# The state-space stage of a four-stage layer chain: one activation table set, the token sum on GpSimd, and five call lists in a new order

## The reference

```python
A = -jnp.exp(A_log)
zxbcdt = u @ W_in.T
z = zxbcdt[..., :D_INNER]
xBC = zxbcdt[..., D_INNER:D_INNER + CONV_DIM]
dt = jax.nn.softplus(zxbcdt[..., D_INNER + CONV_DIM:] + dt_bias)
xBC = _silu(conv over 4 tokens of xBC + conv_b)
...
xs = x * dt;  Ad = A * dt
Y_diag = einsum(C, B, exp(segsum(Ad)), xs)
states = running state, decayed by exp(cumsum(Ad)), plus B, xs
y = Y_diag + Y_off + x * D
y = y * _silu(z)
y = y * lax.rsqrt(jnp.mean(y * y, axis=-1, keepdims=True) + EPS) * norm_w
return y @ W_out.T
```

## Time and profile before

| what | value |
|---|---|
| median of 3 runs | 1187.65 us |
| lowest and highest | 1184.77 and 1187.85 us |
| the profiled execution: time | 1185.47 us |
| its span in the trace | 1183.4 us |
| PE busy in the span | 1045.4 us, 88% |
| DVE | 959.9 us, 81% |
| ACT | 893.4 us, 75% |
| POOL | 738.1 us, 62% |
| first layer, start to end | 0 to 359.8 us |

### The profile page before, as it was taken

One profiled execution on the slowest core, in us unless ns is written; L12 is line 12 of the kernel. 1 busy time (PEld: TensorE's weight loads), 2 busy tenths in 40 slices (PEclk: granted clock), 3 DMA queues, 4 the chain that ended last, 5 costly groups with the idle time before them and its releaser, 6 DMA issues. The chain is left out here.

```text
span 1183.4 us, 17445 instructions
## 1 busy us (share of the span) xinstructions
PE 1045.4 (88%) x5234; PEld 698.0 (59%) x5234; DVE 959.9 (81%) x1319; ACT 893.4 (75%) x1697; POOL 738.1 (62%) x638
## 2 busy tenths in 40 slices
PE   5999999999968999998476599999999999988987
PEld 4677677676753334444245357667575766756576
DVE  5999999999962576545689989999999999999741
ACT  7878787887644455556777889999898999986743
POOL 1546554654560443534568997979889897988420
PEclk9999999999998999999678899999999999999899
DMA  4543434323405001112866546556565565645201
GB/s 128 153 135 109 122 104 130 112 82 114 126 29 180 1 18 54 37 36 91 211 137 172 123 136 150 143 135 149 151 143 139 151 158 135 148 133 142 67 5 36
DMA packets 93232, 133.83 MB, mean 113 GB/s; under 512 B 8786, under 2 KB 47698, under 8 KB 93140
## 3 DMA queue, kind: packets, MB, share of 16 engines
q1 hardware_dynamic: 93140, 132.73, 41.6%
HBM read 116.45 MB, written 14.16 MB: 110 GB/s over the span
## 5 line engine op out<-in xcount | busy, mean ns | idle before, releaser
L2219 DVE TENSOR_TENSOR_SCAN state<-bank_a,h,state 128x512 f32<-128x512 f32 x256 | 316.4, 1270 | 27.5 <-POOL state L2489 12.4
L2489 POOL TENSOR_TENSOR state<-uc,Bb 128x1024 f32<-128x1024 f32 x64 | 150.7, 2367 | 35.3 <-DVE prod L2225 25.9
L2489 POOL TENSOR_TENSOR state<-s,Bb 128x1024 f32<-128x1024 f32 x64 | 150.7, 2367 | 28.2 <-DVE prod L2225 19.7
L1654 PE MATMUL bank_y<-ident,prod 128*128 128x128 f32 x1024 | 138.5, 282 | 28.5 <-DVE prod L2225 28.4
L1654 PEld LDWEIGHTS bank_y<-ident,prod 128*128 128x128 f32 x1024 | 122.8, 145 | 68.3 <-DVE prod L2225 35.8
L2225 DVE TENSOR_TENSOR prod<-state,bank_c 128x1024 f32<-128x1024 f32 x128 | 154.2, 1204 | 6.4 <-ACT bank_c L1875 4.2
L1699 PE MATMUL bank_m<-w,f_h 128*128 128x256 f32 x448 | 106.1, 387 | 0.0
L39 PE MATMUL bank_m<-nT,w 128*128 128x512 f32 x224 | 103.8, 602 | 0.9 <-ACT nT L1953 0.9
L1870 ACT ACTIVATE bank_a<-s,A 128x512 f32<-128x512 f32 x128 | 86.2, 680 | 12.6 <-DVE state L2219 12.5
L1870 ACT ACTIVATE bank_a<-dtc,A 128x512 f32<-128x512 f32 x128 | 86.4, 681 | 10.4 <-DVE state L2219 10.2
L1699 PEld LDWEIGHTS bank_m<-w,f_h 128*128 128x128 f32 x448 | 83.5, 192 | 15.8 <-issue 5.8
(11 more groups left out here) (388 smaller groups left out, 2595.9 us busy)
## 6 DMA issues: line engine op xcount, KB each, us to landing
Bb<-CB_rows SPq DMA_DIRECT2D x128, 256.0 KB, 4.1
Cb<-CB_rows SPq DMA_DIRECT2D x128, 256.0 KB, 4.7
abc<-decays SPq DMA_DIRECT2D x32, 512.0 KB, 4.7
Ebc<-ramps SPq DMA_DIRECT2D x64, 128.0 KB, 3.2
uT<-in_uT SPq DMA_DIRECT2D x8, 512.0 KB, 4.3
u<-in_u SPq DMA_DIRECT2D x8, 512.0 KB, 4.3
x_tokens<-x2s SPq DMA_DIRECT2D x8, 512.0 KB, 2.9
x_rows<-x1T SPq DMA_DIRECT2D x8, 512.0 KB, 2.7
```

Of the source, the lines that this page charges most:

```text
L1654: i = e.matmul(p_y[c // 2][:, at:at + P], prod[n % 2][:, k, c * CH:(c + 1) * CH], ident[:, :], start=False, stop=(n == NS - 1), is_transpo ...
L2219: e.tensor_tensor_scan(s[:, k, :], p_a[k][:, :], s[:, k, :], h0[:, n, k:k + 1], ALU.mult, ALU.add).then_inc(v_s, 1)
L2489: e.tensor_tensor(state[at % 3][:, :, :], uc[b % 2][:, :, :], both(Bb[n % 4][:, :]), ALU.mult).then_inc(p_b, 1)
```

## The change

Three things are done.

1. Table sets. ACT names one set that has both Exp and Ln, `EXP_LN`, ahead of the first Exp and in `row_exp` of every later block. The set for Exp alone that `row_decay(0)` asked for is gone. Between `row_exp(b)` and `row_decay(b)` no silu is called.
2. Token sum. `add_tokens` moves from DVE to POOL: x1T's blocks 0 and 1 are added into a new tensor `held` (128x2x512), then each of the blocks 2 to 6 onto it: six additions of 128x1024. DVE sums `held` over its tokens once, at the end (`sum_tokens`). `parts` has two columns.
3. Order. The lists of all five engines are written in another order, at the start, in the loop and at the end.

```diff
+EXP_LN = "natural_log_exp_and_others"
...
-        parts = sb("parts", [P, KD, NB])
+        parts = sb("parts", [P, KD, 2])
...
-            zeros = a("zeros", [P, CH])
+            zeros, held = a("zeros", [P, CH]), a("held", [P, KD, TB])
...
                 def row_exp(b):
+                    if b > 0:
+                        e.preload_act_table_set(EXP_LN)
                     e.wait_ge(s_row, 6 * b + 2)
...
                     if b == 0:
-                        e.preload_act_table_set("exp_and_others")
                         e.wait_ge(v_negA, 1)
...
                 e.wait_ge(ld_col, DMAS)
+                e.preload_act_table_set(EXP_LN)
                 e.activation(negA[:, :], vec_at["A_log"], ACT.Exp).then_inc(a_negA, 1)
...
-                def add_tokens(b):
-                    e.wait_ge(a_tx, NC * (b + 1))
-                    e.reduce_sum(parts[:, :, b], x1T[:, :, b * TB:(b + 1) * TB], mybir.AxisListType.X)
-
...
+                def sum_tokens():
+                    e.wait_ge(p_sum, NB - 2)
+                    e.reduce_sum(parts[:, :, 0], held[:, :, :], mybir.AxisListType.X)
...
             def pool(e):
+                def add_tokens(b):
+                    e.wait_ge(a_tx, NC * (b + 1))
+                    after(e, p_sum, b - 1)
+                    e.sem_inc(step, 1)
+                    one = x1T[:, :, 0:TB] if b == 1 else held[:, :, :]
+                    e.tensor_tensor(held[:, :, :], one, x1T[:, :, b * TB:(b + 1) * TB], ALU.add).then_inc(p_sum, 1)
+
...
-                    e.reduce_sum(parts[:, :, NB - 1], x1T[:, :, tokens(NB - 1)], mybir.AxisListType.X).then_inc(c_w, 1)
+                    e.reduce_sum(parts[:, :, 1], x1T[:, :, tokens(NB - 1)], mybir.AxisListType.X).then_inc(c_w, 1)
```

More of the change, by code:

```diff
@@ L397, in tensor @@
                         within(post, 0)
-                    if live(last):
-                        project_out(last, 3)
+                    if live(old):
+                        turn_out(old, 2)
+                    if live(post):
+                        prepare(post, 1)
                     if live(old):
@@ L408, in tensor @@
                         project(it, 4)
+                    if live(last):
+                        project_out(last, 3)
                     if live(post):
@@ L595, in scalar @@
+                for it in range(NB + 3):
+                    old, last, post = it - 3, it - 2, it - 1
+                    if live(last):
+                        spread_S(last, 1)
+                    if 0 < post < NB:
+                        row_decay(post)
+                    if live(last):
+                        direct(last, 2)
+                        evac_B(last, 2)
                     if 0 < post < NB:
-                        evac_conv(post, 0)
-                        row_exp(post)
@@ L626, in vector @@
+                    if live(post):
+                        square(post, 0)
             def vector(e):
@@ L761, in vector @@
                 decays(0, 0)
-                for it in range(NB + 4):
-                    older, last, post = it - 4, it - 2, it - 1
+                for it in range(NB + 2):
+                    last, post = it - 2, it - 1
+                    if 0 < post < NB:
+                        conv(post, 3)
+                    if live(last):
+                        inputs(last, 2)
+                        mask(last, 2)
+                        mean_square(last, 0)
+                    if 0 < post < NB:
+                        ramps(post)
+                        conv(post, 4)
                     if live(last):
                         residual(last, 0)
+                        gate(last, 2)
+                        decays(last, 3)
                         state(last, 2)
-                        gate(last, 2)
                         inputs(last, 3)
+                        mean_square(last, 1)
                         mask(last, 3)
@@ L932, in pool @@
                     if live(last):
-                        ramped(last, 3)
+                        decayed(last, 2)
                         root(last, 0)
                         squares(last, 1)
+                        state(last, 2)
+                    if 0 < older < NB - 1:
+                        add_tokens(older)
+                    if live(last):
+                        ramped(last, 3)
                         decayed(last, 3)
```

291 lines of the change are left out of this document (131 added, 160 removed).

## The result

| | before | after |
|---|---|---|
| median (4 runs each) | 1187.75 us | 1158.6 us |
| lowest and highest | 1184.77 to 1188.06 | 1157.24 to 1161.4 |
| span of the profiled execution | 1183.4 | 1157.9 |
| soft_err of block 1 begins | 51.48 | 44.83 |
| from there to soft_err of block 7 | 245.7 | 226.9 |

The ratio is 0.9765, 95% interval 0.9745 to 0.9785. In the two traces the layer ends 25.4 us earlier and the spans differ by 25.5: all of the gain is in the first layer.

What follows compares the result with a forecast made beforehand. DVE was taken to bound the kernel, with PE full at 38.4 us a block. Middle 8.1, start 3.7 and end 1.3 us sum to 13.1 us off the 1187.65 us median: 1174.5 us, range 1166 to 1186.

Steps and rivals of the forecast that it cites:

- step 4: New order, middle blocks: 1.2 us of new waits on DVE's 38.40; block 39.6 us, six blocks 8.1 us less.
- PE's floor of 38.4 us: PE's work in a block, scaled from its busy share: losses on DVE shorten the block only to 38.4 us.
- Step 1: Token sum leaves DVE for POOL: 1.12 us a call, five calls on a full DVE, 5.6 us.
- Step 2: 16 fewer table loads on ACT, 20.5 us of its time; not taken off the forecast, as ACT isn't the bound.
- Step 3: Two DVE calls stretched by POOL: ramps freed, 0.79 us a block; soft_err gains 0.36, between 0 and 0.69.
- three points of meeting: New DVE waits at decays (0.8 us), mean_square (0 to 0.5) and residual (0 to 1); 1.2 a block taken.
- Step 5: Layer's start: PE's second projection no longer waits for W_l and starts near 11.5; 3.7 us gained, ends 2 and 5.
- Step 6: Layer's end, after 297: gains less 1.3 for POOL's addition of block 5 and 0.3; 1.3 us, ends -2 and +4.
- Waits did not eat the gain: Rival, middle blocks: waits up to 2.65 us take all won there, leaving 5.0 us: 1182.6 us; chance 0.17.
- the lock lengthened neither call: Rival: ramps, soft_err or either meet a whole 2.36 us POOL instruction; 14.2 us lost, 1188.7 us; chance 0.06.
- POOL came no later than DVE could wait for: Rival: POOL's addition makes xd and low_u late, between state(b,2) and decayed(b,3); 18.5 us lost, 1193 us; chance 0.05.
- PE is really the bound: Rival, middle blocks: new waits only near 0.2 us, block 38.6, 6 us more gained: 1168.5 us; chance 0.12.

Runs made afterwards that it cites:

- gap_drain: Changed kernel with low_u where POOL's addition stood, the addition ahead of decayed(last,1), and blocks 5 and 6 summed by DVE: 1153.48 us, ratio 0.9734.
- order_only: Changed kernel's order on all five engines, but with the old table sets and the token sum on DVE: 1166.25 us, ratio 0.9836.
- old_start_dve: Changed kernel with only DVE's opening list put back to that of the kernel before: 1160.18 us.
- after_again: The changed kernel executed once more, nothing changed: 1158.44 us, ratio 0.9771.
- lowu_late: Kernel before with one POOL call, low_u, moved behind squares(last,2), away from soft_err: 1198.88 us.

## Why the prediction was wrong

The direction was right, and the mechanism mostly; the forecast of 13.1 us was less than half of it. In the traces the layer ends 25.4 us earlier, 12.3 more than the sum: 10.7 more in the six blocks, 2.95 more at the start, 1.3 less at the end. The step that failed is step 4, the new order. By the steps:

- **What bounds the kernel.** DVE leads: shown by the runs, its busy time and the block fall together. PE's floor of 38.4 us was too high by 0.9 to 1.0: gap_drain has blocks of 37.42 and 37.53 us. I had taken its busy share for work that can't be made shorter. Before, PE shows 38.72 us busy in a block of 41.05, and in gap_drain 37.42 for the same work; what the difference is was not tried. What told the floor was the added 0.45 us and the shorter block. The 30 us of the earlier trace rows are also not a whole block: scaled up they gave ACT 35.1 and POOL 26.3 us, where the block itself has 33.79 and 23.42. The Trainium skill (Perfetto Trace Analysis, Identifying the Most-Contended Engine) calls matmul busy time no good measure of how near a kernel is to its roofline and wants the weight loads' busy share beside it; the traces agree: for the same work PE's busy time differs by 1.3 us between the block before and gap_drain's, and PEld's by 0.4 (29.11 and 29.52).
- **Step 1, the sum.** 1.12 us a call left DVE, as said. The block gained 0.55, since POOL's chain to xd then becomes what DVE waits for: 0.69 us, forecast 0.8. The point is right.
- **Step 2, the table sets.** 16 loads fewer, and I put the time at nothing. Nearly so in the old order (0.16 us a block, 0.6 at the layer's end). In the new one they are worth 4.2 us: 0.4 to 0.5 in each block from 3 on, by a way that I had not seen (ACT's earlier square moves a POOL call out of soft_err's way), and 2.2 in block 1, where DVE then does not wait for PE. ACT's idle time did not cover the loads, as I had said that it would.
- **Step 3, the lock.** ramps 0.47 everywhere, 0.8 gained, as said. soft_err: I took the middle of 0 and 0.69; it was all of it, 0.7. My reading that the stretched calls are those whose inputs all lie in SBUF was too wide: it takes two such inputs (below).
- **Step 4, the new order; this is the step that failed.** I took 1.2 us of new waits a block from three points of meeting. Only the first is in the trace (0.69 us). project_out and the root behind the squares cost nothing. The list itself is also shorter than I counted. The block came out 1.63 us under my 39.6. By DVE's start-to-start times: 0.51 for the waits not met, 0.35 for soft_err, 0.18 because the waits of before were 0.56 and not the 0.38 that I subtracted, 0.05 for ramps and all other calls together, and 0.53 for zs, mv and xs calls, whose successors start sooner in the new order with calls of unchanged length. I had no term for this last; order_only has it too, so it belongs to the order, but what makes it was not tried. Six blocks by 1.63, and 0.9 more because the first of them is shorter still, make the 10.7 us between my 237.6 and 226.9.
- **Step 5, the start.** 3.7 said, 6.65 measured. I had counted PE's second projection, which waited for W_l, and it did start at 11.29 as forecast. But old_start_dve has that start too and loses 3.7 us, because DVE's first conv stood behind the third W_l. That DVE and ACT together gave 3.9, close to my 3.7, is luck. What I missed besides is SP's order, 1.9 us: I had looked at the queues for the loops and not for block 0.
- **Step 6, the end.** 1.3 said, nothing measured in the profile after, 1.1 in after_again, where the clock did not fall at 316. The term of 1.3 for the addition of block 5 was wrong: DVE's last state comes no sooner without it, so the gains that I set against it came out smaller as well. Which of them was not tried.
- **The rivals.** Waits did not eat the gain, the lock lengthened neither call in the changed kernel, POOL came no later than DVE could wait for. "PE is really the bound" was right to expect fewer waits than 1.2 us (0.2, measured 0.69), but its block of 38.6 us rests on the same floor, and that is why my range ended at 1166.
- **Median and span.** The medians differ by 29.1 us, the spans by 25.5; the profiled execution of before was 2.3 under its median, and that of the changed kernel 1.1 above its own, the 1.1 us of the lower clock. The 25.4 are all in the first layer, though not every part of them has a cause here; the rest is the scatter of single executions (3 to 4 us between the lowest and the highest of each kernel).

## What to carry to other kernels

Before you call an engine full by its busy share, add a known piece of work to it, and see how much of it the time shows; a floor set too high cuts off the good side of a range. Measure the added piece in place: I took it for 0.6 us, and it was 0.45. When calls move between hand-written lists, lay the lists of the two engines beside each other between two points where one waits for the other: a call is free only behind the hand-over that the other engine waits for, and the end of a turn is not such a place if the next turn opens with that hand-over. Parts measured alone add up to nothing where they only work together: here the sum and the tables took nothing off the layer in the old order, and 8 us in the new.

## What the runs showed of the hardware

- In the loop two DVE calls read two SBUF tensors, soft_err and ramps. When they start inside a POOL call on SBUF tensors they end no sooner than 0.15 us (soft_err) or 0.28 us (ramps) after it, however short they are: 0.27 becomes 0.65 us behind a 0.72 us POOL call, and 0.48 becomes 2.35 behind one of 2.38. The short neighbours count as well as the long ones. Calls with one SBUF input keep their length: st (0.43 us) with up to 1.9 us of the POOL call still to come, and the token sum (1.19 to 1.20 us) in order_only. The Trainium skill (SBUF — State Buffer, SBUF: two separate sides) describes this as an exclusive lock for the whole instruction, and the traces agree.
- Taking such an overlap away by moving the POOL call cost 13 us where the move put the call ahead of one that DVE waits for (lowu_late, at a granted clock of 0.92 over 89 us).
- PE's granted clock can differ between two executions of one kernel that were in step until then. It fell to 0.61 and 0.53 in the 4 us from 316 on in the profile after and stayed at 1.00 in after_again; PE had idled 1.86 and 1.76 us ahead of 314.9 and 314.8. Sixteen matmuls took 1.91 us in the one and 1.04 in the other, and the layer's end came 1.1 us later.
- 0.45 us of small matmuls (16 of 128*32 by 128x128) added to PE at 99.6% busy (37.82 of 37.97 us) cost no time; added to a block of 37.52 us they made it 37.96.
